# Who issues the transfer of the negated row maxima, and in which pairs the experts' weights are loaded

## What is computed

```
x  = hidden;  xn = layernorm(x)
Q, K, V = low-rank projections of layernorm(xn) (+ bias)
attn    = softmax(causal(Q K^T / sqrt(8)));  ctx = attn V
h       = xn + ctx @ out_U @ out_V + out_b
attention part = h + mlp(layernorm(h))
expert part    = sum over the top 2 of 9 experts: (silu(xn Wg) * (xn Wu)) Wd, weighted
result  = x + attention part + expert part
```

## Time and profile before

| what | value |
| --- | --- |
| median of three runs | 1042.43 us |
| profiled execution | 1045.36 us, its span 1043.6 us |
| attention loop in it | about 98 to 624 us |
| TensorE busy, share of the span | 94% |
| VectorE, ScalarE, GpSimd busy | 67%, 52%, 41% |
| mean granted TensorE clock | 0.955 |

### The profile page before, as it was taken

How to read it: one execution, slowest core, us unless ns; L and a number is a source line. 1 busy time by engine, 2 the same in 40 slices (tenths; PEclk the granted TensorE clock), 3 DMA queues, 4 the chain that set the end, 5 groups by cost and what they waited for, 6 DMA issues and landing times. The chain is left out here.

```text
span 1043.6 us, 25266 instructions
## 1 busy us (share of the span) xinstructions
PE 975.9 (94%) x7701; PEld 756.9 (73%) x7701; DVE 702.6 (67%) x3192; ACT 538.1 (52%) x1256; POOL 431.4 (41%) x563
## 2 busy tenths in 40 slices
PE   4768999999999999999999997999999999999997
PEld 4536565666666665666666656999999999998896
DVE  5647588877778666777777863555555554557887
ACT  1552255555555545555555573555555555564442
POOL 9462122144444444454555431544545444441100
PEclk9685799999999999999999997999999999999999
DMA  8284355335445335444443314222222222238784
GB/s 232 83 225 159 125 183 175 104 113 164 130 128 139 118 97 143 130 127 120 134 125 111 95 33 112 67 62 65 62 66 63 67 70 61 74 95 236 215 233 132
DMA packets 133558, 127.13 MB, mean 122 GB/s; under 512 B 17274, under 2 KB 113652, under 8 KB 133428
## 3 DMA queue, kind: packets, MB, share of 16 engines
q1 hardware_dynamic: 109860, 67.83, 23.7%
q0 software_dynamic: 20592, 56.43, 17.2%
q10 hardware_dynamic: 2976, 1.26, 0.5%
HBM read 57.15 MB, written 42.60 MB: 96 GB/s over the span
## 5 line engine op out<-in xcount | busy, mean ns | idle before, releaser
L1393 DVE CUSTOM_DVE_ANT_0 att_masked_st<-att_m_ps,att_mask_st 128x128 bf16<-128x128 f32 (+1 forms) x1024 | 312.9, 353 | 120.3 <-PE att_m_ps L999 86.9
L817 ACT ACTIVATE att_probs<-att_t_ps 128x512 f32<-128x512 f32 x384 | 229.3, 598 | 223.3 <-PE att_t_ps L1023 201.6
L1641 POOL DMA_INDIRECT y_scratch<-moe_y,moe_row_now x136 | 132.6, 975 | 153.5 <-DVE moe_y L1895 96.9
L652 POOL DMA_INDIRECT slot_x<-att_xs,att_slot_now x128 | 125.8, 983 | 159.3 <-PE att_t_ps L1023 134.9
L1889 DVE TENSOR_TENSOR moe_hidden<-moe_gate,moe_up_ps 128x352 f32<-128x352 f32 x136 | 70.9, 521 | 109.7 <-issue 80.0
L1023 PE MATMUL att_t_ps<-att_mask_ts,att_ident_b 128*128 128x256 bf16 (+1 forms) x384 | 125.2, 326 | 0.0
L1718 PE MATMUL moe_y_ps<-w_down,moe_hidden_t 128*128 (+1 forms) x816 | 114.2, 276 | 1.8 <-issue 1.2
L1816 ACT ACTIVATE moe_gate<-moe_gate_ps 128x352 f32<-128x352 f32 x136 | 63.1, 464 | 95.9 <-PE moe_up_ps L1701 95.9
L1718 PEld LDWEIGHTS moe_y_ps<-w_down,moe_hidden_t 128*128 128x128 f32 (+1 forms) x816 | 101.8, 191 | 3.8 <-issue 3.6
L1022 PE MATMUL att_t_ps<-att_odd_stack,att_k_stack 97*128 97x512 f32 x192 | 81.4, 425 | 6.8 <-DMA att_odd_stack<-att_neg_max 6.2
L1022 PE MATMUL att_t_ps<-even_stack,att_k_stack 97*128 97x512 f32 x192 | 82.9, 432 | 4.3 <-DMA even_stack<-att_neg_max 4.1
(11 more groups left out here) (264 smaller groups left out, 2081.8 us busy)
## 6 DMA issues: line engine op xcount, KB each, us to landing
att_k_stack<-att_qk_parts POOLq DMA_DIRECT2D x96, 128.0 KB
slot_x<-att_xs POOLq DMA_DIRECT2D x17, 516.0 KB, 3.3
moe_x<-slot_x SPq DMA_DIRECT2D x34, 258.0 KB, 2.8
att_xs<-xn_scratch SPq DMA_DIRECT2D x32, 256.0 KB
mlp_rows<-y_scratch POOLq DMA_DIRECT2D x16, 512.0 KB, 5.7
even_stack<-att_qk_parts SPq DMA_DIRECT2D x192, 32.0 KB
att_odd_stack<-att_qk_parts SPq DMA_DIRECT2D x192, 32.0 KB
xn_scratch<-att_probs POOLq DMA_DIRECT2D x16, 256.0 KB, 3.0
```

Of the source, the lines that this page charges most:

```text
L652: pool.indirect_dma_start(env["slot_x"][:], bass.IndirectOffsetOnAxis(ap=slot_now[c.parity][:, col:col + 1], axis=0), xs[c.parity][:, t, k ...
L817: act.activation(probs[:, m % PT, :], t_ps[m % 2][:], ACT.Exp).then_inc(exp_done, 1)
L1393: last = dve.tensor_tensor_reduce(out=masked_st[m % 2][:, part], in0=m_ps[m % 2][:, part], in1=mask_st[:, SEQ - width:], scale=1.0, scalar ...
L1641: pool.indirect_dma_start(env["y_dram"][:], bass.IndirectOffsetOnAxis(ap=row_now[q.parity][:, t:t + 1], axis=0), y[c.parity][:], None).the ...
```

## The change

ScalarE issues the transfer of the maxima itself: `copy_max` gets a wait for its own copy and the `dma_start`, with the same tensors, size and completion semaphore. `stack_max` and its three calls go from SP's list. And a table `W_AT` puts a step's loads of weights into pairs 0 and 6 in place of 10 and 11.

```diff
-            if pair >= UNITS - 2 and LATE <= step < LATE + W_STEPS:
-                k = 2 * (step - LATE) + pair - (UNITS - 2)
+            if pair in W_AT and LATE <= step < LATE + W_STEPS:
+                k = 2 * (step - LATE) + W_AT.index(pair)
                 return k if k < W_LOADS else None
...
-        K_SECOND_AT, K_FIRST_AT, BIAS_AT = (1, 2, 3), (8, 9, 10), 7
+        K_SECOND_AT, K_FIRST_AT, BIAS_AT, W_AT = (1, 2, 3), (8, 9, 10), 7, (0, 6)
...
-                def stack_max(c, b):
-                    sp.wait_ge(max_copied, 2 * c.index + b + 1)
-                    sp.dma_start(q_stack[c.parity][ROWS:ROWS + 1, :, :, b * SEQ:(b + 1) * SEQ].bitcast(F32),
-                                 neg_max[b][:].bitcast(F32)).then_inc(max_stacked[b], 16)
-
...
-                    stack_max(p, 1)
                     if not first:
...
                         stack_q(at(half, d + 2), 0)
-                    if not last:
-                        stack_max(at(half, d + 1), 0)
                     if (p.index, 2) in XS_AT:
                         load_xs(at(0, XS_AT[p.index, 2]))
...
-                stack_max(at(0, 0), 0)
...
                     act.mul(neg_max[b][:], free_ps[bank][0:HEADS, 0:SEQ], -1.0).then_inc(max_copied, 1)
+                    act.wait_ge(max_copied, 2 * c.index + b + 1)
+                    act.dma_start(q_stack[c.parity][ROWS:ROWS + 1, :, :, b * SEQ:(b + 1) * SEQ].bitcast(F32),
+                                  neg_max[b][:].bitcast(F32)).then_inc(max_stacked[b], 16)
```

## The result

The changed kernel takes 1049.53 us, median of 5 runs (1046.82 to 1050.23), against 1042.24 us for the kernel before (5 runs): a ratio of 1.0062, 95% interval 1.0041 to 1.0083. It is slower by 0.6%, 16 us above the forecast and above its range. The profiled execution took 1049.53 us, its span 1047.8 us.

The account below looks back on a forecast made before the run. It took TensorE, busy 94% of the span, as the bound. Weights -9.1, clock -1.7, ScalarE issues 0 and xs +1.8 gave -9.0 us against the median: 1033.4 us, range 1028.5 to 1041 us.

Parts of the forecast that it names:

- The weights' term: First scores after steps 3, 4, 6, 7, 8, 10: moving the weight loads removes six waits, -9.1 us.
- the clock's: TensorE's half-clock stretches after two waits, 1.7 us each: neither expected to remain, one counted against the median, -1.7 us.
- The issuer's terms of 0: ScalarE's issue stays hidden before its exponential, and the maxima land as early as from SP: 0 us each.
- what SP does instead: In six steps SP's loads of xs run ahead of the maxima, whose transfer meets them: 0.3 us each, +1.8 us.
- the six places: Ends of steps 2, 3, 4, 10, 11 and 13, where loads of xs stood behind the maxima.
- The tail argument: At those six steps only the end of the xs transfer meets the maxima, so 0.3 us each.
- rival one: Ends of steps 2, 3, 4, 10, 11, 13: xs replaces the weights, costing 4.9 us; 1038.2 us, chance 0.17.
- The upper bound: Most that xs could delay the maxima: 0.82 us per step, from the fill at 158 us; times six, 4.9 us.
- The second: All 32 transfers: maxima land later from ScalarE, 3.2 us per 0.1 us beyond the margin; 1054 us at 0.8, chance 0.09.
- The third: Slots 1 or 13: weights delay another deadline, half a microsecond at each of 15 loads; 1041 us, chance 0.07.
- the prediction's sentence: On ScalarE's own queue the maxima would pass the xs traffic: that term about 0, the sum -10.8 us.

Follow-up runs that it names:

- the pair with either issuer: Two kernels, weights at pairs 0 and 6, loads of xs waiting until the maxima land, differing only in issuer: ScalarE 1034.24 us, SP 1032.42 us.
- the last run: The changed kernel with loads of xs waiting for the landed maxima and weights back at pairs 10 and 11: 1044.11 us, ratio 1.0005.
- the weights alone: The kernel before with only the loads of weights moved to pairs 0 and 6, SP still issuing the maxima: 1032.1 us, ratio 0.9890.
- the run with SP in ScalarE's place: The kernel before with weights at pairs 0 and 6, SP issuing the maxima but behind the loads of xs: 1050.81 us, ratio 1.0068.
- the hold for the landing: The changed kernel with SP's loads of xs waiting until the maxima of b = 0 have landed: 1034.24 us, ratio 0.9905.
- held for the copy: The changed kernel with SP's loads of xs waiting for the copy of the maxima: 1040.0 us, ratio 0.9966.
- issuer alone: The changed kernel with weights back at pairs 10 and 11, ScalarE issuing and loads of xs running ahead: 1061.94 us, ratio 1.0190.

## Why the prediction was wrong

**The weights' term was right in its sum, and partly by luck.** It said -9.1 us of waits and -1.7 us of clock, 10.8 together; alone it measured 1032.1 against 1043.25, 11.2 us. In the profiled executions the waits fell by 5.7 us (10.3 to 4.6) and both clock falls went. The wait part was sized too high, since 0.56 and 0.53 us stayed behind steps 3 and 7 and small ones came elsewhere, and the clock's too low: both falls counted. Two errors of opposite sign met.

**The issuer's terms of 0 held within the noise.** The issue took 0.51 us, the exponential came at 0.64 us behind the copy, and TensorE waited for an exponential once for 0.4 us, as before. For the landing the pair with either issuer differs by less than its intervals, and by the 95% interval of the last run the issuer cost at most 2.8 us with the weights at their old places.

**The step that failed is the price of what SP does instead, "+1.8 us".** The place was named to the step, and the price was wrong by a factor of ten: the changed kernel stands 17.4 us above the run with the weights alone. In the profiled pair 11.2 us are waits (15.8 against 4.6; 9.2 of them at the six places) and 6.8 us is half of 13.6 us of clock, 18.0 in sum for a loop that grew by 18.2. That xs did it, and not the issuer, is shown by the run with SP in ScalarE's place (+18.7 us) and by the hold for the landing (all but 2 us back). Two things made the price wrong.
- The tail argument. I called what meets the maxima "the tail of a transfer and not its middle", and rival one was marked down because xs "only reaches its start". My own rows said otherwise: the pair of step 11 filled the machines from 2.0 to 3.5 us behind its first issue, which laid on step 3 is 239.6 to 241.1 us, nearly the whole flight of maxima issued at 239.1 and due at 241.2. In the changed kernel the share was about 1 from 241 to 243 us, 2 to 4 us behind the first issue at 238.90, and the maxima, issued at 240.63, were due at 242.7. The middle met them.
- The upper bound. I took 0.82 us from one fill as the worst that half a megabyte can do. The kernel's own waits behind the weights, up to 1.93 us, were the nearer rows: loads of 144 to 528 KB, issued 0.2 to 1.1 us ahead of the maxima, with a second one mostly behind. Size would not have led there either: the 1.93 us stood where the two loads were the smallest, 192 and 144 KB. Six times 1.9 us would have been 11 us, -9.1 - 1.7 + 11.4, and the range would have reached over no change.

The clock then added to the loss, 6.8 us to 11.2 us of waits: I had reckoned what falls would go with the old waits, and none that new waits of the same length would bring.

**The rivals.** The first, xs in place of the weights, was the mechanism, given 0.17 and 1038.2 us; it was priced with the same bound and so stayed on the wrong side of no change. The second, a later landing from ScalarE, fell as an account of the loss: with SP as issuer the loss is the same. The third, another deadline for the weights, does not show as its sign had it: no run waited for key or query parts. The waits of 1.50 us in step 9 and 1.05 us behind step 6 are again for the maxima, and both are absent with the weights alone; what causes them was not tried.

**The rule weighed against the rows.** That machines take turns between queues packet by packet ("DMA: Bandwidth & Descriptors", section Queues, rings and completion order, in the Trainium skill) would by the prediction's sentence make this term about 0. The runs disagree with that conclusion: on a queue of its own the transfer lost about as much as behind the loads on SP's. Whether the machines take turns they do not show. The other statement of that section, that a completion's semaphore write lands only after all earlier writes of that DMA engine, across its queues, fits the runs: behind step 3 the 16 KB landed only after the half megabyte ahead had passed, with either issuer. That this is the cause, and not the shared machines alone, is not shown; and it leaves open why the landing came 1.7 us after the share had dropped (243.0 and 244.73 us).

## What to carry to other kernels

A wait on an issuing engine is also a gate for all that stands behind it: when an instruction is taken off an ordered queue, list what moves forward in time and whom it will meet. Lay the stretch in which the machines are full, and not only its end, on the flight of the transfer that must land. Price a collision from the longest wait at the same spacing that the trace holds, whatever the size of the load, and add the clock that waits of that length have cost in the same trace. And of two parts that come together, time each alone: here one was worth 11 us and the other hid it.

## What the runs showed of the hardware

- 0.6 us of lead decided. With 512 KB of loads issued 0.6 us behind a 16 KB transfer it landed after 2.1 us at three of the six places and 2.5 to 3.0 us at the others (weights alone, issued by SP); at the same instant after 3.3 to 3.8 us (held for the copy, issued by ScalarE), and TensorE waited 0.9 to 1.4 us; with the first load 1.3 to 1.9 us ahead after 3.5 to 4.5 us (the changed kernel), and it waited 1.1 to 2.2 us.
- The small transfer was late even after the large ones were through: in the changed kernel the DMA share from 243 to 244 us was 0.22, and TensorE went on at 244.79.
- Which of SP and ScalarE issues made little difference to a 16 KB transfer: 0.55 and 0.51 us to issue, both 0.03 us behind the copy, and medians of 1032.42 and 1034.24 us with xs held.
- The clock fell to half at waits of 1.60 and 1.93 us before the change and of 1.73, 1.84 and 2.15 us with it, and not at others of 1.54, 1.73 and 1.96 us. The length of the wait does not decide: in the experiments it fell behind waits of 1.30 us (issuer alone), 1.37 us (xs held for the copy) and 1.38 us (issuer alone, xs held for the landing), and not behind one of 2.41 us (issuer alone). What does is open.
